# A mixture-of-experts block with attention: products of the identity ahead of the first work, and a new order of the first expert preparations

## The reference

```python
x = x + 0.5 * ffn(layernorm(x)); x = x + attn(layernorm(x)); x = x + 0.5 * ffn(layernorm(x))
def ffn(x):                       # x: 2048 x 256
    probs = softmax(x @ router_w.T)
    w = top_p_weights(probs, 0.9)  # kept while the sum of the larger ones is not over 0.9
    for e in range(8):
        y = (silu(x @ gate_w[e].T) * (x @ up_w[e].T)) @ down_w[e].T
        out = out + y * w[:, e:e + 1]
# attn: 16 heads of 16, 4 key heads, rms norm and rotation of q and k, causal softmax, output projection
```

## Time and profile before

| | us |
|---|---|
| median of 3 runs | 1164.2 |
| profiled execution, span from the first to the last instruction | 1162.9 |
| TensorE busy | 1140.2 (98%) |
| VectorE busy | 804.0 (69%) |
| GpSimd busy | 668.5 (57%) |
| ScalarE busy | 575.3 (49%) |

### The profile page before, as it was taken

How to read it: one execution, slowest core, us unless ns; L and a number is a source line. 1 busy time by engine, 2 the same in 40 slices (tenths; PEclk the granted TensorE clock), 3 DMA queues, 4 the chain that set the end, 5 groups by cost and what they waited for, 6 DMA issues and landing times.

```text
span 1162.9 us, 23008 instructions
## 1 busy us (share of the span) xinstructions
PE 1140.2 (98%) x8161; PEld 688.5 (59%) x8161; DVE 804.0 (69%) x1993; ACT 575.3 (49%) x954; POOL 668.5 (57%) x737
## 2 busy tenths in 40 slices
PE   5899999999999999999999999999999999999998
PEld 2466555665565665665665666665656666656565
DVE  7878887678788677677677777767767455554443
ACT  4545544444555655555555555555455554333332
POOL 4545444368387677668667668658656464332322
PEclk9999999999999999999999999999999999999999
DMA  5411210000000000000000000000000000000000
GB/s 182 130 56 55 73 51 1 1 1 2 1 1 2 1 2 2 1 1 1 2 1 1 1 1 2 10 10 1 1 2 5 15 2 1 1 19 1 1 1 19
DMA packets 10109, 19.25 MB, mean 17 GB/s; under 512 B 2192, under 2 KB 6800, under 8 KB 10000
## 3 DMA queue, kind: packets, MB, share of 16 engines
q1 hardware_dynamic: 10000, 17.80, 4.7%
HBM read 15.70 MB, written 2.10 MB: 15 GB/s over the span
## 4 chain that ended last, share of the span: by engine, by line
PE 89%; DVE 0%; issue 0%; DVEq 0%
PE YB L330 27%; PE G L311 26%; PE U L311 26%; PE S L490 2%; PE S L467 2%; PE S L397 1%; PE S L505 1%; PE S L441 1%; PE S L407 1%; PE S L449 1%; PE S L378 0%; PE S L435 0%; PE S L499 0%; PE S L386 0%; PE S L417 0%; PE S L330 0%
## 5 line engine op out<-in xcount | busy, mean ns | idle before, releaser
L1103 POOL TENSOR_TENSOR HS<-TS,HS 128x512 f16<-128x512 f32 x256 | 300.4, 1173 | 396.6 <-ACT HS L564 395.6
L311 PE MATMUL G<-XS,W 128*128 128x512 f16 x1536 | 376.3, 381 | 0.9 <-ACT XS L594 0.9
L330 PE MATMUL YB<-W,HS 128*128 128x256 f16 x3036 | 373.8, 273 | 3.3 <-DVE X L748 2.6
L311 PE MATMUL U<-XS,W 128*128 128x512 f16 x1536 | 375.0, 380 | 0.8 <-DVE W L833 0.8
L727 DVE SCALAR_TENSOR_TENSOR TS<-TS,G 128x512 f32<-128x512 f32 x256 | 175.2, 684 | 241.9 <-ACT TS L557 241.7
L330 PEld LDWEIGHTS YB<-W,HS 128*128 128x128 f16 x3036 | 289.9, 98 | 75.1 <-DVE X L748 5.9
L564 ACT ACTIVATE HS<-TS 128x512 f16<-128x512 f32 x256 | 161.0, 629 | 250.9 <-DVE TS L732 250.5
L557 ACT ACTIVATE TS<-G,TSC 128x512 f32<-128x512 f32 x256 | 175.5, 686 | 209.9 <-PE G L311 202.7
L311 PEld LDWEIGHTS U<-XS,W 128*128 128x128 f16 x1536 | 150.7, 98 | 183.8 <-issue 2.7
L311 PEld LDWEIGHTS G<-XS,W 128*128 128x128 f16 x1536 | 146.6, 98 | 134.8 <-issue 2.9
L732 DVE SCALAR_TENSOR_TENSOR TS<-TS,U 128x512 f32<-128x512 f32 x256 | 176.0, 687 | 29.6 <-DVE TS L727 2.3
(11 more groups left out here) (178 smaller groups left out, 840.4 us busy)
## 6 DMA issues: line engine op xcount, KB each, us to landing
room<-in_gate SPq DMA_DIRECT2D x4, 512.0 KB, 3.2
room<-in_up SPq DMA_DIRECT2D x4, 512.0 KB, 3.3
room<-in_down SPq DMA_DIRECT2D x4, 512.0 KB, 3.9
QKT<-in_gate SPq DMA_DIRECT2D x4, 512.0 KB, 3.8
QKT<-in_up SPq DMA_DIRECT2D x4, 512.0 KB, 3.4
QKT<-in_down SPq DMA_DIRECT2D x4, 512.0 KB, 4.1
out_y<-X SPq DMA_DIRECT2D x16, 128.0 KB, 1.7
X<-in_x SPq DMA_DIRECT2D x3, 512.0 KB, 5.8
```

What stands on the lines that cost most here:

```text
L311: mm = eng.matmul(bank[:, :], W[:, e, wl, jj, kk * I + m * P:kk * I + (m + 1) * P], flat(XS16[:, b % 2, xl, kk, :, :], 'cq'), start=q == 0 ...
L330: mm = eng.matmul(out, HS[:, j % 2, hl, kk, m * P:(m + 1) * P], W[:, e, wl, 2, kk * D:(kk + 1) * D], start=kk + hl + wl == 0, stop=kk == K ...
L1103: eng.tensor_tensor(HS[:, j % 2, 1, m, :], TS[:, k % 3, :], HS[:, j % 2, 0, m, :], ALU.subtract).then_inc(L['g_lo'].sem, 1)
```

## The change

It has five parts. TensorE multiplies the identity by itself (128 columns, into U1, whose contents nobody reads) 40 times before its first work and 23 times between the steps of the start. The broadcast of up's maximum (second part of expert 0's scale) stands ahead of the transposes of the fourth tile, not behind them. VectorE computes the low half of expert 0's up directly behind that of gate, ahead of the statistics of block 1. The transposes of tiles 4 and 5 (the second block's) stand in slot 4, not 3. The preparation of expert 1 starts in slot 3, not 0, that of expert 2 in slot 12, not 8.

```diff
-PREP = [-99, 0, 8, 24, 36, 47, 58, 72, 83]
+PREP = [-99, 3, 12, 24, 36, 47, 58, 72, 83]
-FTP0 = (3, 3, 6, 6)
+FTP0 = (4, 4, 6, 6)
+        def pe_warm(eng, n):
+
+            for _ in range(n):
+                eng.matmul(UB[1][:, 0:P], ident16[:, :], ident16[:, :], start=True, stop=True)
# @block.vector
             dve_scale0(eng, 1)
             dve_lo(eng, 0, 0)
+            dve_lo(eng, 0, 1)
             for f in range(BT, 2 * BT):
                 dve_f_stats(eng, f)
...
-            dve_lo(eng, 0, 1)
             for s in range(SLOTS + 1):
                 dve_slot(eng, s)
# @block.tensor
             give_credit(eng, 'p_')
+            eng.wait_ge(s_i2, 1)
+            pe_warm(eng, 40)
             eng.wait_ge(s_i1, 5)
             pe_wt0(eng, 0)
+            pe_warm(eng, 4)
             pe_wb0(eng, 0)
             for f in range(BT - 1):
+                pe_warm(eng, 3)
                 pe_ftp(eng, f, FTP[0])
             pe_wt0(eng, 1)
-            pe_ftp(eng, BT - 1, FTP[0])
+            pe_warm(eng, 4)
             pe_wb0(eng, 1)
+            pe_ftp(eng, BT - 1, FTP[0])
+            pe_warm(eng, 6)
```

More of the change, by code:

```diff
@@ L1401, in _ @@
             give_credit(eng, 'p_')
+            eng.wait_ge(s_i2, 1)
+            pe_warm(eng, 40)
             eng.wait_ge(s_i1, 5)
             pe_wt0(eng, 0)
+            pe_warm(eng, 4)
             pe_wb0(eng, 0)
             for f in range(BT - 1):
+                pe_warm(eng, 3)
                 pe_ftp(eng, f, FTP[0])
             pe_wt0(eng, 1)
+            pe_warm(eng, 4)
+            pe_wb0(eng, 1)
             pe_ftp(eng, BT - 1, FTP[0])
-            pe_wb0(eng, 1)
+            pe_warm(eng, 6)
             for s in range(SLOTS):
```

## The result

| | before | after |
|---|---|---|
| median, us | 1164.47 (8 runs, 1164.08 to 1165.06) | 1167.72 (8 runs, 1166.81 to 1169.31) |
| ratio to before | | 1.003, 95% interval 1.002 to 1.004 |
| span of the profiled execution | 1162.9 | 1165.7 |

The forecast was 1163.8, with a range to 1166.0; the change costs 3.3 us. The profiled execution of after took 1167.9, 2.2 us more than its span. The distance was 2.1 to 2.3 in every later run too, so I estimate that the profiled execution of before took 1165.1, 0.6 above its median: 2.8 us of difference in span and 3.3 in the medians are the same loss.

The account below looks back on a forecast made before the run. TensorE was taken as the bound, so only the start's shift of gate's product of quarter step 9, 60.42 to 60.0, counts: 1162.9 - 0.4 + 1.3 = 1163.8 us. The 8-in-10 range was 1161.5 to 1166.0.

Parts of the forecast that it names:

- The bound, and the instant to forecast: TensorE bounds; only the start counts: the instant it stops waiting, gate's product of quarter step 9 (60.42 before).
- First part, the products: TensorE's start: 40 identity products cost 0 to 0.1 us, 23 cost 0 to 0.4; they give 0 to 0.6, taken as nothing.
- rival D: Start: the identity products do not raise the clock at all; worth 0 to 0.6 us, within the forecast; no chance given.
- Second part: VectorE's start: earlier broadcast gains 0.7 us (0.3 to 0.9); up's low half from 15.1, low halves ready 2.2 earlier.
- Third part: VectorE and ScalarE, block 1's start: normalisations to 21.4 and 25.6; second VectorE product of quarter step 2 gains 1.8 us.
- Fourth part: Two maxima (2.3 us) leave; one (1.13) precedes down's scale; gate's product of quarter step 4 gains 0.7, bounds 0.2 and 1.2.
- What is late next, the clock: TensorE idles 5.7 us before gate's product of quarter step 4, which starts at 1.2 GHz; loss 2.0 us (1.5 to 2.4).
- Rival A: Clock stays up through the pause, or the pause is shorter: time 1161.8 to 1162.8 us; chance 0.23.
- B: Clock stays low longer from gate's product of quarter step 4: 5.0 in place of 2.0 us, time 1166.0 to 1167.6; chance 0.13.
- C: Start bound by something priced at nothing: gate's product of quarter step 4 moves 2 us or more, time 1161 to 1162; chance 0.10.
- From G4 to G9: VectorE's chain sheds 3.5 us, then GpSimd takes over; gate's product of quarter step 9 at 60.0 (59.2 to 60.8).
- Sum: Whole kernel: 1162.9 - 0.4 + 1.3 = 1163.8 us, with 1.3 outside the span; own range 1162.8 to 1164.8.

Follow-up runs that it names:

- w(1) behind lo(7): Changed kernel with GpSimd's low half of expert 1's down behind its low half of step 7: 1166.34 us; other kernels also use this order.
- the three repairs: Changed kernel, normalisations ahead of maxima, 80 identity products in the pause before G4, GpSimd's low half of expert 1's down behind step 7's: 1164.09 us.
- the single run: Kernel before with only the preparations moved, expert 1 from slot 0 to 3 and expert 2 from 8 to 12: 1166.9 us, ratio 1.0019.
- the later pair of runs: The three repairs with the 80 identity products before G4, 1164.09 us, and without them, 1165.56 us.
- w(1) behind lo(8): The three repairs with GpSimd's low half of expert 1's down in slot 19, not 17: 1162.84 us, ratio 0.9984 to the kernel before.
- first try: Kernel before plus early broadcast, early up low half, 63 products, 40 before G2, GpSimd's low half of expert 1's down behind step 7's: 1164.29 us.
- w(1) behind lo(9): The three repairs with GpSimd's low half of expert 1's down in slot 21: 1164.13 us, ratio 0.9995 to the kernel before.

## Why the prediction was wrong

**The bound, and the instant to forecast.** Right. G9 is 2.02 later, the span 2.8. In the runs in which G9 comes early, however, it was not "the instant from which TensorE no longer waits": with w(1) behind lo(7) up to 1.15 went again at y(5).

**First part, the products.** "I take nothing": right, 1164.38 against 1164.53. Whether they raise the clock at G0 (rival D) differs between executions: of the 13 profiles with the 63 products G0 takes 1.47 in five and 2.25 to 2.74 in eight, that of after among these. No run leaves out the transposes, so what they count for the clock stays open.

**Second part.** The broadcast and the scale came nearly as forecast, 12.59 and 13.00, but up's low half at 15.79, not 15.1, behind ScalarE's high half, so that t(0) and h(0) were 0.64 later than forecast (18.84 for 18.2). This too looks like a collision, though no run tests it. The second pair of the very first normalisations stands beside GpSimd's split of the rows; it took 1.07 at 8.33 before and 1.72 in the profile of after. With the three repairs, whose start has the same instructions, it took 1.07, and up's low half and t(0) (18.17) came when forecast. The first row is of after, the other two of the three repairs:

```profile
8.40 1.72 DVE L869 TENSOR_SCALAR W<-X,MVF,RSF 128x256 f32<-128x256 f32 x2
```
```profile
8.56 1.07 DVE L873 TENSOR_SCALAR W<-X,MVF,RSF 128x256 f32<-128x256 f32 x2
...
15.09 1.32 DVE L842 SCALAR_TENSOR_TENSOR W<-room,SCW,W 128x1024 f16<-128x1024 f32 x1 [0.66 <-ACT W L580]
```

The pair takes 1.72 in the same eight profiles in which G0 is slow, and 1.07 in the other five and in all four without the products. What decides between the two is open.

**Third part, the step that failed.** The term that was mis-sized is "the first two normalisations to 21.4" and "two normalisations (25.6)": they were priced at 0.65 a pair, from a row of before in which GpSimd was idle (19.65). Moved a slot, each pair lies beside a lo pass and takes 1.39 and 1.32. (What stands before tanh(1) are the splits of these rows, at 22.46, not their copies, which stand before tanh(2), at 28.74.) By the rows: 0.64 late from the start, the first pair ends at 22.7, 1.3 late; h(1) at 25.3, 1.4 late; the second pair at 27.6, 2.0 late; t(2) at 30.42 for 28.7, 1.7 late. The 1.76 by which G4 misses 35.15 is thus 0.6 from the start and 0.6 to 0.7 from each collision, less 0.1 elsewhere. The run with the normalisations first shows the collision as the cause of the long rows; how much of G4's delay it makes is worked out from the rows above. The error was avoidable: the prediction used the same collision for the router's subtraction, and did not ask it of the rows that the change moved. All eight normalisations of the first two blocks together went from 3.3 to 5.2 us, 0.65 of it in the pair at 8.40 and 1.25 in the two moved pairs (groups of the line by shape, of before and of after: total, mean ns of one, idle before):

```profile
L864 DVE TENSOR_SCALAR W<-X,MVF,RSF 128x256 f32<-128x256 f32 x8 | 3.3, 448 | 0.0
```
```profile
L869 DVE TENSOR_SCALAR W<-X,MVF,RSF 128x256 f32<-128x256 f32 x8 | 5.2, 684 | 0.0
```

The Trainium skill, SBUF — State Buffer, section "Who interferes with whom", names `tensor_scalar`, besides work with two SBUF inputs, among what can contend with GpSimd for the shared ports, and says that `tensor_reduce` never does. The traces agree: in the run with the normalisations first, the maximum at 55.87 took 1.21 us beside w(1) (56.11 to 58.23), as long as those that stand alone.

**Fourth part.** The maximum between h(2) and the scale of down is there (31.81, 1.21), and the copies start 1.06 later than before. As the single run shows, this part carries 2.4 of the 3.3 us, since it puts the maximum before G4, the low clock behind it and w(1) before lo(7). These three the prediction had; what it did not have is how little the leaving maxima give back (0.13 at t(2) in that run).

**What is late next, the clock.** Right, in place and size: pause 5.4 (forecast 5.7), G4 in 2.74. The prediction took 2.0. In the profiled execution of after it is 4.46 from G4 to y(0) (36.91 to 41.37), against 2.60 before (35.84 to 38.44) and 0.1 for the transposed maximum between: 1.8. In the later pair of runs it was 1.9 to 2.2 on TensorE and 1.5 in the time. Rival A, for which the clock stays up, is out. So is B: it was back by 41, 4 us after G4 started. That the measured time lies beside B's 1166.0 to 1167.6 is chance. C is out as well, since G4 came later, not 2 us earlier. The experiments add that a pause far shorter can do it: 2.29 us before G4 in the run with the preparations alone.

**From G4 to G9.** Every named step is there: the subtraction takes 0.19 instead of 1.61 (49.23), y(3) does not wait, w(1) stands between rank and lo(7), and y(4)'s last product waits 1.98 for it. From G4 to G9 I had 24.85 (60.0 less 35.15, with 2.1 for w(1)) and it was 25.53: the rank starts 0.7 nearer to G4 (18.59 for 19.25), takes 3.1 in place of 2.2, since its third pass stands beside VectorE's low half of expert 1, w(1) takes 2.12, and G9 starts 0.6 behind lo(7), not 0.15. The 3.10 of w(1) before held 1.1 beside a low half on VectorE (48.40 to 49.94), so 2.1 was the value to take.

**Sum.** Forecast of G9 60.0, measured 62.44: 1.76 before G4, 0.68 behind it. Another 0.8 of the span comes after G9 (0.4 by 129.61, where before had 127.17, and 0.4 near 270: a wait of 0.82 for a lo pass at 276.59, which six of the 17 profiles have), which I had carried at nothing. So of the 3.2 us by which the span missed its forecast, 1.2 are the two collisions of the third part, 0.6 the one at the start, 0.7 the way from G4 to G9 and 0.8 what follows, less 0.1 elsewhere. The median missed by 0.7 more: the 1.3 us that the forecast adds for what lies outside the span set a median beside the profile of a slower execution, and the distance is 2.1 to 2.3. The range to 1166.0 had its upper end from B, a longer low clock, with every start time on the path exact; a range for G4 of 0.2 to 1.2 gain had no end on the other side of zero.

## What to carry to other kernels

When instructions are moved, ask of each not only what it costs where it stood but what the other engines do at its new place: a VectorE step that reads two operands or scales a copy from SBUF may take the length of GpSimd's pass instead of its own. An idle time is worth filling where TensorE is about to become the bound (80 products before G4 gave 1.5 us, 63 at the start nothing). And an off-path pass on GpSimd should be laid where VectorE reduces or reads PSUM: beside w(1) a maximum kept its 1.21, and h its 0.69 (61.66 with w(1) behind lo(8)). One pass moved by one step was worth 1.3 us.

## What the runs showed of the hardware that I had not expected

A small VectorE step of 0.12 to 0.19 us can take the rest of a GpSimd pass: 1.76 (first try) and 1.95 (three repairs) for the row weight, 1.03 for a 3x3 diagonal, 1.93 for a step of a scale (w(1) behind lo(9)). The blocking goes both ways: a rank pass on GpSimd took 1.66 for 0.73 beside a low half on VectorE.

The same kernel, with products before G4, gave two groups of times, 2.5 us apart: eight runs at 1166.0 to 1166.4 and three at 1168.7 to 1169.0. The profile of one of the three has the clock low from about 62 us, behind a wait of 1.98 us; in the profile of the changed kernel G9 took 1.46 behind the same wait.

The record of the granted clock can be at odds with the pace: G0 took 2.88 us for six products at a recorded 1.00 before, where G4 took 1.47 at the same reading.
